# A new place for every operation in the steps of nine pipelined layers

## The reference

```python
x = x + tanh(g_xattn[0]) * L0_xattn(LN(x), ctx, ctx, mask_bf0, Wq, Wk, Wv, Wo)  # A0: 16 heads of 64, causal mask
x = x + tanh(g_ffn[0])   * L0_ffn(LN(x), w_gate, w_up, w_down)   # F0: 128->512, quantised rows, ternary weights, silu(gate)*up
x = x + tanh(g_xattn[1]) * L1_xattn(LN(x), ctx, ctx, mask_ik0, ...)  # A1: 16 heads of 8, masked
x = x + tanh(g_ffn[1])   * L1_ffn(LN(x), Wg, W1, b1, W2, b2)     # ROUTE, MOE: 8 experts, 2 a token, capacity 269 rows, gelu
x = x + tanh(g_xattn[2]) * L2_xattn(LN(x), ctx, ctx, lens, lens, W, b)   # A2: one head of 128
x = x + tanh(g_ffn[2])   * L2_ffn(LN(x), W_fc, ln_w, ln_b, W_proj)       # F2: ternary, exact gelu, layer norm on the hidden row
x = x + tanh(g_xattn[3]) * L3_xattn(LN(x), ctx, ctx, ...)        # A3: 16 heads of 8, biases, no mask
x = x + tanh(g_ffn[3])   * L3_ffn(LN(x), norm1_w, w1, act_scale, act_bias, norm2_w, w2)  # F3: quantised, relu squared
```

## Time and profile before

| | |
|---|---|
| median of 3 runs | 580.78 us (579.97 to 581.94) |
| the profiled execution | 578.77 us |
| its span | 577.0 us |
| mean granted TensorE clock | 0.907 |
| TensorE busy | 437.9 us (76%) |
| ScalarE busy | 298.5 us (52%) |
| VectorE busy | 294.2 us (51%) |
| GpSimd busy | 153.2 us (27%) |
| chain that ended last | PE 51%, ACT 15%, DVE 14%, issue 9%, POOL 7%, DMA 3% |

### The profile page before, as it was taken

One profiled execution on the slowest core, in us unless ns is written; L12 is line 12 of the kernel. 1 busy time (PEld: TensorE's weight loads), 2 busy tenths in 40 slices (PEclk: granted clock), 3 DMA queues, 4 the chain that ended last, 5 costly groups with the idle time before them and its releaser, 6 DMA issues.

```text
span 577.0 us, 9810 instructions
## 1 busy us (share of the span) xinstructions
PE 437.9 (76%) x3484; PEld 317.8 (55%) x3484; DVE 294.2 (51%) x871; ACT 298.5 (52%) x813; POOL 153.2 (27%) x264
## 2 busy tenths in 40 slices
PE   3798968988886687787887579924766878989932
PEld 2576757767765554454555269912454545655521
DVE  3255456647557535654444442133444335777984
ACT  2354335445544446664665143303567888788832
POOL 4080101101101101123334600058853222322220
PEclk9998989999999888998999579965689999999965
DMA  8950000000000030000000124111000000000000
GB/s 356 384 194 2 1 0 1 1 2 2 1 2 1 1 109 2 1 2 10 11 10 10 37 78 139 37 35 32 19 1 0 1 2 1 2 2 1 2 1 37
DMA packets 7134, 22.09 MB, mean 38 GB/s; under 512 B 1215, under 2 KB 3503, under 8 KB 6575
## 3 DMA queue, kind: packets, MB, share of 16 engines
q1 hardware_dynamic: 6063, 19.37, 9.4%
q0 software_dynamic: 1024, 2.10, 1.2%
HBM read 14.58 MB, written 6.88 MB: 37 GB/s over the span
## 4 chain that ended last, share of the span: by engine, by line
PE 51%; ACT 15%; DVE 14%; issue 9%; POOL 7%; DMA 3%; SPq 0%; POOLq 0%; DVEq 0%; ACTq 0%
PE bank L804 7%; PE bank L852 6%; PE bank L811 5%; ACT prob L551 4%; PE bank L984 4%; DVE mx L1171 4%; PE bank L790 3%; PE bank L975 3%; PE bank L870 3%; PE bank L778 3%; PE bank L820 2%; PE bank L847 2%; PE bank L832 2%; POOL moe_rows L473 2%; PE bank L950 2%
## 5 line engine op out<-in xcount | busy, mean ns | idle before, releaser
L551 ACT ACTIVATE prob<-bank,mx 128x128 f32<-128x128 f32 x384 | 109.8, 379 | 69.5 <-DVE mx L1171 69.1
L1171 DVE TENSOR_REDUCE mx<-bank 128x4 f32<-128x512 f32 x96 | 65.1, 688 | 92.5 <-PE bank L804 79.1
L432 POOL TENSOR_SCALAR rstd<-mv 128x1 f32<-128x1 f32 x64 | 14.1, 221 | 310.1 <-DVE mv L1150 307.8
L535 ACT ACTIVATE probT<-bank 128x512 f32<-128x512 f32 (+1 forms) x104 | 60.4, 581 | 40.3 <-PE bank L811 39.3
L804 PE MATMUL bank<-kz,qz 128*128 128x512 f32 x128 | 69.7, 627 | 3.8 <-ACT prob L551 3.8
L811 PE MATMUL bank<-pack,prob 128*128 128x128 f32 x384 | 61.3, 284 | 5.0 <-ACT prob L551 3.6
L811 PEld LDWEIGHTS bank<-pack,prob 128*128 128x128 f32 x384 | 46.7, 147 | 27.9 <-issue 17.5
L434 POOL TENSOR_TENSOR rstd<-rstd,minus_half 128x1 f32<-128x1 f32 x72 | 42.2, 587 | 6.0
L535 ACT ACTIVATE xnT<-bank 128x128 f32<-128x128 f32 x48 | 13.3, 276 | 53.1 <-PE bank L769 53.1
L820 PEld LDWEIGHTS bank<-va,probT 128*128 128x128 f32 x256 | 32.3, 195 | 4.0 <-issue 3.9
L453 POOL TENSOR_SCALAR xn<-pack,mv,rstd 128x128 f32<-128x128 f32 x40 | 32.6, 816 | 7.1 <-POOL rstd L434 6.9
(11 more groups left out here) (218 smaller groups left out, 905.3 us busy)
## 6 DMA issues: line engine op xcount, KB each, us to landing
yrows_d<-moe_rows SPq DMA_DIRECT2D x2, 1510.0 KB, 21.6
pack<-pack_d SPq DMA_DIRECT2D x1, 2112.0 KB, 15.7
expert<-experts_d SPq DMA_DIRECT2D x4, 514.0 KB, 9.1
pack<-experts_d SPq DMA_DIRECT2D x4, 514.0 KB, 4.2
pack<-pack_d SPq DMA_DIRECT2D x1, 2048.0 KB, 10.4
xrows_d<-moe_rows SPq DMA_DIRECT2D x1, 1080.0 KB, 21.3
moe_rows<-xrows_d SPq DMA_DIRECT2D x8, 135.0 KB, 3.4
yrows_d<-o_n SPq DMA_DIRECT2D x8, 135.0 KB, 1.8
```

The source lines that it names most:

```text
L535: act.activation(dst, src, ACT.Identity if kw else ACT.Copy, **kw).then_inc(E[layer][name].sem, 1)
L551: act.activation(prob[:, g % 2, P * j:P * j + P], bank[S_BANK[g % 2]][:, P * j:P * j + P], ACT.Exp, bias=mx[:, g % 2, j:j + 1]).then_inc(E ...
L1171: dve.tensor_reduce(mx[:, g % 2, :], bank[S_BANK[g % 2]][:, :].rearrange("p (h t) -> p h t", h=GH), AX.X, ALU.max, negate=True).then_inc(E ...
```

## The change

`LAG` changes for F0 (2 to 1) and F2 (2 to 3); the number of steps stays. In the tables of GpSimd, ScalarE, TensorE and VectorE nearly every entry of every layer but MOE gets another slot, another place in it, or another lag. The functions, tiles, banks and waits are not edited. The diff of the tables:

```diff
-LAG = [2, 2, 3, 1, 2, 4, 2, 3, 2]
+LAG = [2, 1, 3, 1, 2, 4, 3, 3, 2]
...
# GpSimd
                 A0: [
                     [],
                     [],
-                    [None, (0, rs, A0)],
-                    []],
+                    [],
+                    [(0, rs, A0)]],
...
                 A1: [
                     [],
-                    [],
-                    [],
-                    [(0, rs, A1)]],
+                    [(0, rs, A1)],
+                    [],
+                    []],
                 ROUTE: [
                     [],
                     [],
-                    [(0, rs, ROUTE)],
-                    [(1, scatter)]],
+                    [(0, rs, ROUTE), None, (1, scatter)],
+                    []],
                 A2: [
-                    [],
-                    [],
-                    [(0, rs, A2)],
-                    [(0, fetch_ahead)]],
+                    [(2, rs, A2)],
+                    [],
+                    [(2, fetch_ahead)],
+                    []],
                 F2: [
-                    [],
-                    [None, (0, rs, F2)],
-                    [(1, rs_hid)],
-                    []],
+                    [(3, rs_hid)],
+                    [],
+                    [],
+                    [None, (1, rs, F2)]],
                 A3: [
-                    [None, (0, rs, A3)],
+                    [(1, rs, A3)],
...
                 F3: [
                     [],
-                    [(0, rs, F3), (1, rms_hid)],
-                    [],
-                    []],
+                    [],
+                    [],
+                    [None, (2, rms_hid), (0, rs, F3)]],
...
# ScalarE
             def attention(layer):
                 return [
-                    [(2, exps, layer, 3), (2, probsT_sb, layer, 2)],
-                    [(1, exps, layer, 0), None, (2, probsT_sb, layer, 3)],
+                    [(2, exps, layer, 3), (1, v_sb, layer), (2, probsT_sb, layer, 2)],
+                    [(1, exps, layer, 0), None, None, None, None, (2, probsT_sb, layer, 3)],
                     [(1, exps, layer, 1), (1, probsT_sb, layer, 0), (0, xt_sb, layer)],
-                    [(1, exps, layer, 2), (1, probsT_sb, layer, 1), (0, q_sb, layer), (0, v_sb, layer)]]
+                    [None, (1, exps, layer, 2), None, (1, probsT_sb, layer, 1), (0, q_sb, layer)]]
...
                 A0: [
-                    [(1, exps, A0, 0), (0, k_sb, 0), None, (2, probsT_sb, A0, 3)],
-                    [(1, exps, A0, 1), (0, k_sb, 1), (0, xt_sb, A0), (1, probsT_sb, A0, 0)],
-                    [(1, exps, A0, 2), None, (1, probsT_sb, A0, 1), (0, q_sb0, 0)],
-                    [(1, exps, A0, 3), (1, probsT_sb, A0, 2), (0, q_sb0, 1)]],
+                    [(2, exps, A0, 3), None, (0, k_sb, 0), (1, exps, A0, 0), (2, probsT_sb, A0, 3), (0, k_sb, 1)],
+                    [(1, exps, A0, 1), (0, xt_sb, A0), (1, probsT_sb, A0, 0)],
+                    [(1, probsT_sb, A0, 1), (1, exps, A0, 2), None, (0, q_sb0, 0), (1, probsT_sb, A0, 2)],
+                    [(0, q_sb0, 1)]],
                 F0: [
                     [],
                     [],
-                    [None, (0, xq_sb, F0), None, None, None, (1, hq_sb, F0)],
-                    [None, None, (0, tanh_gate)]],
+                    [None, (0, xq_sb, F0)],
+                    [None, (1, hq_sb, F0), (0, tanh_gate)]],
...
-                    [None, (0, xt_sb, ROUTE)],
+                    [(0, xt_sb, ROUTE)],
...
                 A2: [
-                    [None, None, (1, xt_sb, A2), (2, exps2)],
-                    [],
-                    [(3, ot_sb, A2), (2, probsT_sb2)],
-                    []],
+                    [],
+                    [None, (1, xt_sb, A2), None, None, (2, probsT_sb2)],
+                    [(3, ot_sb, A2)],
+                    [(1, exps2)]],
                 F2: [
                     [],
-                    [(1, gelu2), (2, hT_sb2)],
-                    [],
-                    [(0, xt_sb, F2)]],
+                    [None, (1, gelu2)],
+                    [(2, hT_sb2)],
+                    [None, None, (0, xt_sb, F2)]],
...
                 F3: [
                     [(1, relu3)],
-                    [(1, sumsq3), None, (2, hq_sb, F3)],
-                    [],
+                    [(1, sumsq3)],
+                    [(2, hq_sb, F3)],
                     [None, (0, xq_sb, F3)]],
...
# TensorE
             def attention(layer):
                 return [
-                    [(1, scores, layer, 0), (2, probsT, layer, 2), (2, pv, layer, 1)],
-                    [(3, y, layer), None, (1, scores, layer, 1), (2, probsT, layer, 3), (2, pv, layer, 2)],
-                    [(1, scores, layer, 2), (1, probsT, layer, 0), (0, xt, layer), (2, pv, layer, 3)],
-                    [(1, scores, layer, 3), (1, probsT, layer, 1), (0, q, layer), (0, v, layer), (1, pv, layer, 0)]]
+                    [(1, scores, layer, 0), (2, probsT, layer, 2)],
+                    [(3, y, layer), None, None, (1, scores, layer, 1), (2, pv, layer, 1), (2, pv, layer, 2), (2, probsT, layer, 3)],
+                    [(1, scores, layer, 2), (2, pv, layer, 3), (1, probsT, layer, 0), None, (0, xt, layer)],
+                    [(1, scores, layer, 3), None, None, None, None, None, (1, probsT, layer, 1), (0, q, layer), (1, pv, layer, 0), (0, v, layer)]]
...
                 A0: [
-                    [(1, scores0, 0), (2, probsT, A0, 3), (0, proj0, "k", 0), (2, pv0, 2)],
+                    [(1, scores0, 0), (0, proj0, "k", 0), (2, pv0, 2), (2, probsT, A0, 3)],
                     [(0, proj0, "k", 1), (1, probsT, A0, 0), (2, pv0, 3), (0, xt, A0), (2, ot0, 0), (0, proj0, "v", 0)],
-                    [(1, scores0, 1), (1, probsT, A0, 1), (2, ot0, 1), (1, pv0, 0), (0, proj0, "q", 0)],
-                    [None, (1, probsT, A0, 2), (0, proj0, "v", 1), (1, pv0, 1), (0, proj0, "q", 1), (2, y0)]],
+                    [(1, probsT, A0, 1), (1, scores0, 1), None, (2, ot0, 1), (1, pv0, 0), (0, proj0, "q", 0)],
+                    [(0, proj0, "v", 1), (1, probsT, A0, 2), (0, proj0, "q", 1), (1, pv0, 1), (2, y0)]],
                 F0: [
-                    [(2, y_ffn, F0, tern["downT"]), (1, up, F0, "up", tern["upT"][:, :], xqT)],
+                    [(1, up, F0, "up", tern["upT"][:, :], xqT)],
                     [],
                     [None, None, (0, xt, F0), None, (1, ht, F0)],
-                    [None, None, None, None, (0, up, F0, "gate", tern["gateT"][:, :], xqT)]],
+                    [None, None, None, None, (0, up, F0, "gate", tern["gateT"][:, :], xqT), (1, y_ffn, F0, tern["downT"])]],
...
                 ROUTE: [
-                    [(1, logits)],
-                    [None, None, (1, places)],
+                    [],
+                    [(1, logits), None, None, None, None, (1, places)],
...
                 A2: [
                     [],
-                    [(2, probsT2)],
-                    [(3, ot2)],
-                    [None, (2, pv2), (1, scores2), (0, xt, A2), (3, y, A2)]],
+                    [(4, y, A2), (1, xt, A2), None, (1, scores2), (3, ot2), (2, probsT2)],
+                    [],
+                    [(2, pv2)]],
                 F2: [
+                    [],
                     [(1, up, F2, "up", tern["fcT"][:, :], xnT[1])],
                     [(2, ht, F2)],
-                    [None, (2, y_ffn, F2, projw)],
-                    [(0, xt, F2)]],
+                    [(2, y_ffn, F2, projw), (0, xt, F2)]],
...
                     [(1, up, F3, "up", tern["w1T"][:, :], xqT)],
-                    [None, None, (2, ht, F3)],
-                    [(2, y_ffn, F3, tern["w2T"])],
-                    [None, (0, xt, F3)]],
+                    [],
+                    [(2, ht, F3)],
+                    [(2, y_ffn, F3, tern["w2T"]), None, (0, xt, F3)]],
...
# VectorE
             def attention(layer):
                 return [
-                    [(1, top_of, layer, 0), (0, ln_stats, layer)],
-                    [(1, top_of, layer, 1), (3, resid, layer)],
-                    [(1, top_of, layer, 2)],
-                    [(1, top_of, layer, 3), (2, norm, layer)]]
+                    [(2, top_of, layer, 3), None, (0, ln_stats, layer), None, (1, top_of, layer, 0)],
+                    [None, None, (1, top_of, layer, 1), (3, resid, layer)],
+                    [None, None, (1, top_of, layer, 2)],
+                    [(2, norm, layer)]]
...
                 A0: [
-                    [(1, top_of, A0, 0), (1, top_of, A0, 1), (0, ln_stats, A0), (2, norm0, 2)],
-                    [(2, norm0, 3), None, (2, ot_sb0, 0), (0, v_sb, 0)],
-                    [(1, top_of, A0, 2), (1, top_of, A0, 3), (0, weights), (2, ot_sb0, 1), (1, norm0, 0)],
-                    [(0, v_sb, 1), (1, norm0, 1), (2, resid, A0)]],
+                    [(2, norm0, 1), (1, top_of, A0, 0), (0, ln_stats, A0), (2, norm0, 2), (1, top_of, A0, 1)],
```

(59 more changed lines are left out.)

1 line of the change is left out of this document (removed).

## The result

The change takes the kernel from 580.92 us to **498.61 us** (median of 4 runs, 497.46 to 498.97); the ratio is 0.8579, 95% interval 0.8559 to 0.8600. The span went from 577.0 to 496.7 us, by 80.3; the working had 71 and took 12 back.

What follows compares the result with a forecast made beforehand. Limits differ by stretch: mostly TensorE, with waits in the handover and GpSimd at phase 3's start. Profiled 578.8 us less 71 of removed waits plus 12 for unseen ones gave 519.8, put at 521 with the median's 2.0; range 502 to 556.

Steps and rivals of the forecast that it cites:

- the allowance: Over some 36 changed steps, small waits the hand walk did not look for: 0.33 us each, 12 us added back.
- the handover: A0 to A1, steps 8 and 9: fewer waits through VectorE's new order, 41.5 to 33.5 us, -8; bounds 31 and 37.
- the walk's 18 us: Phase 3, by following the new order: -5 at its start, then -6, -3 and -4 us.
- A1 with F0: Steps 10 to 12: y_ffn's waits for vz shrink as v_sb moves and F0's chain runs one lag ahead, -8 us.
- A0 with F0: Steps 2 to 7: TensorE's brackets go, full steps take 18.4 us, 108.6 against 133.7 in all, -25 us.
- A1 with ROUTE: Steps 13 to 17: waits of places and A1's xt go; -9.5 in three steps, -2.5 in the last two, -12 us.
- Start of phase 3: Steps 0 to 8: the last token sum no longer stands behind A2's resid, -5 us, bounds 0 and 6.
- The table loads: Steps 9 to 12, ScalarE: each counts as its row's 1.28 us, without the skill page's drain; supports -6 us.
- three signs of being wrong: Score or mask bracket over 1 us for exps; VectorE idle over 1 us before L1247; A0's granted clock falling.
- That A1 and A3 would not gain: Rival: moving group 3's exps and maximum into the next step makes A1's and A3's steps wait; about 549 us, chance 0.29.
- Slower: Rival: gate0 at the head of VectorE's step waits for tanh and delays phase 1's steps; about 588 us, chance 0.05.
- To the letter: Rival: the hand walk holds without the 12 us for unseen waits, handover 2 us better; about 507 us, chance 0.06.

Runs made afterwards that it cites:

- experiment 1: Kernel before with only the new tables and lag of A0, F0, A1 and ROUTE; A2, F2, A3 and F3 old: 517.12 us.
- experiment 4: Kernel after with A0's exps(3) back in ScalarE's slot 3, ahead of q_sb0(1), hq_sb and tanh: 507.20 us.
- experiment 5: Kernel after with ROUTE's old order on TensorE and VectorE, places a turn later than in the kernel before: 506.15 us.
- experiment 8: Kernel after with F0's y_ffn and resid_q back at the head of the next step, LAG of F0 2: 522.63 us.
- experiment 10: Kernel after with top(3) of A1 and A3 back in VectorE's slot 3 of its own step, ahead of norm: 502.47 us.
- experiment 11: Kernel after with gate0 back in slot 3 of VectorE's own step, ahead of resid_q: 504.50 us.
- experiment 3: Kernel after with weights ahead of ot_sb0(1) on VectorE again, in A0's slot 2: 512.53 us.
- experiment 2: Kernel before with only the new tables of A0 and F0 and F0's lag of 1; A1 and ROUTE old as well: 553.72 us.
- experiment 9: Kernel before with only F0's y_ffn and resid_q moved to the end of their own step, LAG of F0 1: 576.63 us.
- experiment 6: Kernel after with v_sb of A1 and A3 back behind q_sb in ScalarE's slot 3: 500.94 us.
- experiment 7: Kernel after with F3's hq3 in VectorE's slot 1 and scale3 in slot 2, the old order: 503.61 us.

## Why the prediction was wrong, and where it was right

The step that failed is the allowance: "over some 36 changed steps I allow 0.33 us each, 12 us". The new order has hardly any such waits where TensorE bounds the step: from 57.5 to 150 us TensorE's timeline has no bracket of 0.25 us or more, and in steps 2 to 15 its idle time is 4.5 us in all. The terms of the walk had room for that already (33.5 for the handover, with 31 for no wait left), so a good part of the 12 us counted them twice. In phase 3 small waits did stay, but the walk's 18 us came in full there as well (20.3, or 18.5 without what experiment 1 puts down to the clock). I took the small brackets of before (0.89, 0.95) for a noise that any order has. Experiments 4, 5, 8, 10 and 11 show that brackets of 0.5 to 2.5 us come and go with the place of one or two entries, and experiment 3 that 0.88 does. Without it the forecast is 509.

Another 9 us (80.3 of span for 71) are sizes, and the last 2 are the step from the profiled execution to the median: I added 2.0, as in before, and after's median is 0.2 below its profiled execution. (519.8 and 2.0 make 521.8; it was put down as 521.) The handover was put at -8 and gave -11.8, A1 with F0 at -8 and gave -11.1. I read the pure work of a step as its length less its brackets. That still has matmuls at 1.2 GHz in it, and time that each wait costs beyond its bracket, at full clock too: the step of A0 with four brackets, 22.5 less 3.55, leaves 18.95, and after without them took 18.15, 0.2 us less for each. So the 0.5 us that I took off the 18.9 was of the right kind and a little small. In both kernels' tables TensorE's busy time falls by 2.9 us in each of these two stretches; the rest is waits, which the new order removes nearly all and not in part.

By part: A0 with F0 was -25 and is -25.3, masks 18.15 us apart for 18.4. A1 with ROUTE -12, is -11.5, and here two misses cancel: the first three steps had -9.5 and gave all of it, and the last two, -2.5 in the sum, gave nothing in this pair of traces (42.13 and 42.15 us). But that stretch differs between traces: 40.8 to 42.1 us in the seven other kernels with the same tables of A1 and ROUTE as after, 44.2 in the two with both old (experiments 2 and 9). So some 2 us may be gained there, and the pair doesn't show it. What bounds the stretch is open; by its sum it is not GpSimd, busy 16.31 and 16.35 us. Start of phase 3 -5, is -5.4, of which 1.8 came in experiment 1 with the old tables; so the tables gave some 3.6. Steps 9 to 12 -6, is -6.8; 13 to 16 -3, is -3.8; the end -4, is -4.4. MOE 0, is -0.1. The table loads cost their row: the steps of 9 to 12 became shorter, 12.4 us each (49.75 for four). The drain that the Trainium skill states ("ScalarE: Activation LUTs", "What ACT_TABLE_LOAD costs"), by which they would have taken about 15 (an estimate from the page's 1.38 us), doesn't show.

Some totals were right for reasons that were not, and so by luck. The bracket before `y0` I put down to `q1`'s earlier place; in experiment 4 `q1` has that place and `y0` waits 0.92, so it is the move of `exps(3)` that removes it, which I had costed at nothing. The bracket before `probsT(3)` I let TensorE's order cover; experiment 9 keeps the old place of `probsT(3)` and loses the bracket all the same, since what was late there was `hid0` behind `resid_q` behind `y_ffn`. The wait for `vz` I put down to `v_sb`; experiment 6 puts `v_sb` back at a price of 2.3, experiment 8 puts `y_ffn` back at 24.

None of the three signs of being wrong came: in A0's steps of after the largest bracket before a mask is 0.67, VectorE has no idle time before L1247, and the granted clock is 1.00.

The rivals. That A1 and A3 would not gain is out: moving top(3) into the next step is worth 3.9 us by itself (experiment 10), of which 1.8 by the traces in the steps with A1. Half of its picture holds in another form: with new tables for A0 and F0 alone, A1's steps 10 to 15 gain nothing (experiment 2). "Slower" rested on `gate0` at the head of the step; experiment 11 shows that place as a gain of 5.9. "To the letter", at 507, was the nearest, and still 8 too high.

What stays open: a move has no price of its own. `y_ffn` with `resid_q` is worth 24 us in the new order and 4.6 in the old one, so no account by move sums to 82; only the one by stretch does. And in phase 3 only two moves were tried backwards (experiments 7 and 10); what of the -6.8 in steps 9 to 12 the new tables of A2 and F2 gave is not shown.

## What to carry to other kernels

When an order is written by hand, ask of each wait which entry ahead of it on the same engine is itself waiting, and who claims the bank next; the copy that looks late is often fine, and its reader early. An operation that waits for another engine (`gate0`, `resid_q`, the exps of the last group) belongs behind those that are ready, even into the next step. And price a wait that lowers the clock above its bracket, and don't put an allowance for unseen waits against an order in which the bounding engine always has something ready.
